# Two heads of a pair in the two 64-row halves of the array, and one VectorE instruction for the maxima of both

## The reference

```python
q = (x @ Wq).reshape(B, S, 16, 16).transpose(0, 2, 1, 3)
c_kv = x @ Wkv_down                                   # latent of 64
k, v = heads(c_kv @ Wk_up), heads(c_kv @ Wv_up)
qf, kf = rope(q), rope(k)
scores = einsum('bhqd,bhkd->bhqk', qf, kf) / sqrt(16)
scores = where(causal, -inf, scores)
out = einsum('bhqk,bhkd->bhqd', softmax(scores), v)
```

## Time and profile before

| | |
|---|---|
| median of 3 runs | 789.13 us (788.01 to 790.67) |
| the profiled execution | 787.88 us, its span 786.1 us |
| TensorE busy (matmul) | 699.7 us, 89% |
| VectorE busy | 567.3 us, 72% |
| ScalarE busy | 397.4 us, 51% |
| 640 row-maximum reductions on VectorE | 346.6 us |
| 640 matmuls for the maxima, 640 for the scores | 237.0 and 244.9 us |
| 1280 records of the values | 134.1 us |

### The profile page before, as it was taken

One profiled execution on the slowest core, in us unless ns is written; L12 is line 12 of the kernel. 1 busy time (PEld: TensorE's weight loads), 2 busy tenths in 40 slices (PEclk: granted clock), 3 DMA queues, 4 the chain that ended last, 5 costly groups with the idle time before them and its releaser, 6 DMA issues.

```text
span 786.1 us, 13117 instructions
## 1 busy us (share of the span) xinstructions
PE 699.7 (89%) x4086; PEld 444.5 (57%) x4087; DVE 567.3 (72%) x1297; ACT 397.4 (51%) x848; POOL 240.3 (31%) x297
## 2 busy tenths in 40 slices
PE   3579899899999999999999999999979999999910
PEld 3456575565665556556654555554467777777710
DVE  6666679778879977787698888863687755555545
ACT  2225365455656666667666776766823232222204
POOL 6526173440072207010611000010147413333332
PEclk9759899899999999999999999999999999999965
DMA  4864315035015101500341265332332223333254
GB/s 138 204 172 109 83 43 148 24 103 119 1 42 148 56 1 41 121 2 1 93 89 65 65 215 189 126 97 57 87 98 102 90 83 95 108 108 108 87 187 160
DMA packets 45096, 75.94 MB, mean 97 GB/s; under 512 B 5695, under 2 KB 23359, under 8 KB 44863
## 3 DMA queue, kind: packets, MB, share of 16 engines
q1 hardware_dynamic: 37423, 57.55, 27.2%
q0 software_dynamic: 4896, 13.67, 5.0%
q10 hardware_dynamic: 2720, 4.00, 1.4%
HBM read 41.91 MB, written 32.93 MB: 95 GB/s over the span
## 4 chain that ended last, share of the span: by engine, by line
PE 70%; DVE 16%; DMA 4%; issue 4%; ACT 3%; ACTq 1%; POOL 0%; SPq 0%; POOLq 0%; DVEq 0%
PE banks_ps L1144 15%; PE banks_ps L1124 14%; PE banks_ps L1085 14%; PE banks_ps L1181 7%; DVE mx L1342 6%; PE banks_ps L1215 5%; PE banks_ps L1001 3%; PE banks_ps L1092 2%; PE banks_ps L1194 2%; DMA q_stack<-m_rows 2%; PE banks_ps L1228 1%; ACT probs L888 1%; PE banks_ps L1277 1%; PE banks_ps L1203 1%; DVE base L1809 1%
## 5 line engine op out<-in xcount | busy, mean ns | idle before, releaser
L1342 DVE TENSOR_REDUCE mx<-banks_ps 128x1 f32<-128x512 f32 (+3 forms) x640 | 346.6, 602 | 93.1 <-PE banks_ps L1085 50.1
L888 ACT ACTIVATE probs<-banks_ps 128x512 f32<-128x512 f32 (+3 forms) x640 | 304.1, 546 | 180.9 <-PE banks_ps L1124 166.6
L1124 PE MATMUL banks_ps<-q_stack,k_stack 98*128 98x512 f32 (+3 forms) x640 | 244.9, 399 | 15.5 <-ACT probs L888 7.2
L1085 PE MATMUL banks_ps<-k_stack,q_stack 96*128 96x512 f32 (+3 forms) x640 | 237.0, 400 | 7.3 <-DMA q_stack<-kq_split 3.4
L1085 PEld LDWEIGHTS banks_ps<-k_stack,q_stack 96*128 96x128 f32 x640 | 124.8, 198 | 82.0 <-DVE mx L1342 37.1
L1124 PEld LDWEIGHTS banks_ps<-q_stack,k_stack 98*128 98x128 f32 x640 | 122.4, 195 | 51.4 <-ACT probs L888 29.1
L741 POOL TENSOR_SCALAR_AFFINE_SELECT probs<-probs 128x512 f32<-128x512 f32 x64 | 41.0, 640 | 331.0 <-ACT probs L888 331.0
L1144 PE MATMUL banks_ps<-probs,v_ones 128*17 128x512 f32 (+3 forms) x1280 | 134.1, 536 | 1.0 <-POOL probs L741 1.0
L798 POOL DMA_INDIRECT token_y<-ys,dest x47 | 45.4, 966 | 79.2 <-DVE ys L1785 76.3
L1144 PEld LDWEIGHTS banks_ps<-probs,v_ones 128*17 128x17 f32 x1280 | 29.5, 97 | 64.9 <-issue 41.1
L1181 PE MATMUL banks_ps<-w_up_sb,xg_t 128*128 x188 | 63.8, 462 | 0.3 <-ACT xg_t L941 0.3
(11 more groups left out here) (186 smaller groups left out, 685.0 us busy)
## 6 DMA issues: line engine op xcount, KB each, us to landing
kq_split<-kq_stage SPq DMA_DIRECT2D x32, 256.0 KB, 3.4
k_stack<-kq_split SPq DMA_DIRECT2D x8, 768.0 KB, 6.6
q_stack<-kq_split SPq DMA_DIRECT2D x32, 192.0 KB, 6.1
xg<-slot_x SPq DMA_DIRECT2D x47, 130.0 KB, 2.1
slot_x<-blank SPq DMA_DIRECT2D x11, 520.0 KB, 6.9
w_up_sb<-w_up SPq DMA_DIRECT2D x16, 352.0 KB
kq_split<-kq_stage SPq DMA_DIRECT2D x32, 128.0 KB, 3.2
x_raw<-xT SPq DMA_DIRECT2D x4, 512.0 KB, 5.7
```

The lines of the kernel that those rows point to most:

```text
L888: nc.scalar.activation(probs[:, s % PROB_BUFS, h, off:CH], score_bank(n)[:, off:CH], ACT.Exp)\
L1085: ins = nc.tensor.matmul(dst[:, at:at + keys], q_stack[0:STACK, u % 4, h, tile * P:(tile + 1) * P], k_stack[0:STACK, pair, kb * CH + k0:kb ...
L1124: nc.tensor.matmul(score_bank(n)[:, off:CH], k_stack[:, 2 * g + h // 2, b * P:(b + 1) * P], q_stack[:, u % 4, h, off:CH], start=True, stop ...
L1342: last = nc.vector.tensor_reduce(mx[:, u % 2, h * TPC + tile, kb:kb + 1], bank_of(bank)[:, at:at + keys], AX.X, ALU.max)
```

## The change

Each head of a pair gets its own half of the partitions: the even head rows 0 to 49, the odd head rows 64 to 113 (48 rows, and 2 for the maximum). `q_stack` loses its zeros. The score matmuls of two neighbouring heads and the two matmuls for the maxima of two heads then use different halves of the array's rows. Banks for the maxima are handed out in pairs: the 576 banks become 288 pairs, each with two of the 4 turn banks; VectorE reduces a pair with one instruction if its two banks are neighbours, and with two if the pair wraps round (bank 3 and bank 0), which 81 of the 288 pairs do, since jobs take one bank and shift the count. A step issues half of its pairs, two scores, half of its jobs, and the same again.

```diff
-STACK = 2 * SPLIT
-ROWS = STACK + 2
+ROWS = SPLIT + 2
+HALF_ROWS = P // 2
...
-        filled.append(filled[-1] + BANKS_A_STEP[u // UNITS_PER_CHUNK])
+        filled.append(filled[-1] + BANKS_A_STEP[u // UNITS_PER_CHUNK] / 2)
...
+        wide = 2 if turn in max_no else 1
+        turn_banks[turn] = [(at + k) % TURN_BANKS if n < first_alone else LAST_MAX_BANKS + at % 2 for k in range(wide)]
+        turn_before[turn] = [user.get(bank) for bank in turn_banks[turn]]
+        user.update((bank, turn) for bank in turn_banks[turn])
+        at += wide
...
-                    sp.dma_start(k_stack[0:STACK, 4 * m:4 * m + 4, c * CH:(c + 1) * CH].bitcast(F32),
-                                 kq_dram[c, n - 1].rearrange("two copy (d j) n -> (two copy d) j n", j=GH)).then_inc(k_stacked, 16)
+                    for par in range(2):
+                        sp.dma_start(k_stack[half_rows(par, SPLIT), 4 * m:4 * m + 4, c * CH:(c + 1) * CH].bitcast(F32),
+                                     kq_dram[c, n - 1, par].rearrange("copy (d j) n -> (copy d) j n", j=GH)).then_inc(k_stacked, 16)
...
-            nc.gpsimd.memset(q_stack[0:STACK, 0:2].bitcast(F32), 0.0).then_inc(zeros_low, 1)
-            link(nc.gpsimd.memset(k_stack[STACK:ROWS, :, 0:CH].bitcast(F32), 1.0))
+            for par in range(2):
+                nc.gpsimd.memset(k_stack[HALF_ROWS * par + 32:HALF_ROWS * par + ROWS, :, 0:CH].bitcast(F32), 1.0).then_inc(ones_set, 1)
...
                 for tile, k0, keys, at in parts:
-                    ins = nc.tensor.matmul(dst[:, at:at + keys], q_stack[0:STACK, u % 4, h, tile * P:(tile + 1) * P],
...
+                    for par in range(2):
+                        ins = nc.tensor.matmul(bank_of(of, par)[:, at:at + keys],
+                                               q_stack[half_rows(par, SPLIT), u % 4, pair, tile * P:(tile + 1) * P],
+                                               k_stack[half_rows(par, SPLIT), stacked, kb * CH + k0:kb * CH + k0 + keys],
...
-                nc.tensor.matmul(score_bank(n)[:, off:CH], k_stack[:, 2 * g + h // 2, b * P:(b + 1) * P],
-                                 q_stack[:, u % 4, h, off:CH], start=True, stop=True).then_inc(pe_scores, 1)
+                nc.tensor.matmul(score_bank(n)[:, off:CH], k_stack[half_rows(h % 2), 2 * g + h // 2, b * P:(b + 1) * P],
+                                 q_stack[half_rows(h % 2), u % 4, h // 2, off:CH], start=True, stop=True).then_inc(pe_scores, 1)
...
-            nc.vector.memset(q_stack[0:STACK, 2:4].bitcast(F32), 0.0).then_inc(zeros_high, 1)
...
+                    b0, b1 = turn_banks[of]
+                    if b1 == b0 + 1:
+                        last = nc.vector.tensor_reduce(mx[:, u % 2, n:other + 1:other - n, kb:kb + 1],
+                                                       turn_ps[:, b0:b1 + 1, at:at + keys], AX.X, ALU.max)
+                    else:
+                        for k, to in enumerate((n, other)):
+                            last = nc.vector.tensor_reduce(mx[:, u % 2, to, kb:kb + 1], bank_of(of, k)[:, at:at + keys], AX.X, ALU.max)
```

More of the change, by code:

```diff
@@ L118, in build_program @@
         at = min(at, first_step[u] - MAX_AHEAD)
-        for bank in reversed(max_banks(u)):
+        for bank in reversed(max_pairs(u)):
             while at >= 0 and len(max_at[at]) >= room(at):
@@ L489, in score_bank, with bank_of, half_rows, mx_row_of @@
             return turn_ps[:, k - SCORE_BANKS]
-        def bank_of(turn):
-            return turn_ps[:, turn_bank[turn]]
+        def bank_of(turn, k=0):
+            return turn_ps[:, turn_banks[turn][k]]
+        def half_rows(par, rows=ROWS):
+            return slice(HALF_ROWS * par, HALF_ROWS * par + rows)
+        def mx_row_of(pair, par, tile):
+            return (par * (GH // 2) + pair) * TPC + tile
         def wait_read(eng, job):
@@ L1153, in run_banks @@
                         max_unit(bank[0])
-                    max_bank(bank)
+                    max_pair(bank)
             def before_scores():
@@ L1165, in _ @@
             for s in range(NS + 1):
-                banks, jobs = quarters(max_at[s]), quarters(aux_at[s], 2)
+                banks, jobs = quarters(max_at[s], 2), quarters(aux_at[s], 2)
                 for half in range(2):
-                    for h in (2 * half, 2 * half + 1):
-                        run_banks(banks[h])
-                        if s < NS:
-                            score_head(s, h)
+                    run_banks(banks[half])
+                    if s < NS:
+                        score_head(s, 2 * half)
+                        score_head(s, 2 * half + 1)
                     for job in jobs[half]:
@@ L1669, in _ @@
             for s in range(NS + 1):
-                banks, jobs = quarters(max_at[s]), quarters(aux_at[s], 2)
-                for k in range(4):
-                    for bank in banks[k]:
-                        reduce_bank(bank)
-                    if k % 2:
-                        for job in jobs[k // 2]:
-                            if job in by_dve:
-                                read_aux(job)
-                    norm_part(s, k)
+                banks, jobs = quarters(max_at[s], 2), quarters(aux_at[s], 2)
+                for half in range(2):
+                    for bank in banks[half]:
+                        reduce_pair(bank)
+                    norm_part(s, 2 * half)
+                    for job in jobs[half]:
+                        if job in by_dve:
+                            read_aux(job)
+                    norm_part(s, 2 * half + 1)
                 for u in range(UNITS):
```

101 lines of the change are left out of this document (48 added, 53 removed).

## The result

The changed kernel takes **878.61 us** (median of 4 runs, 872.86 to 879.11) against 789.62 us of the kernel before (788.01 to 790.67): ratio **1.111** [1.106, 1.116], 89 us slower. The profiled execution has a span of 877.4 us, 91.3 above the 786.1 of before.

The account below looks back on a forecast made before the run. TensorE was taken to set the pace, VectorE 15% behind. Units 8 to 14 -11, units 4 to 7 +2, prologue and units 0 to 3 -3, the rest 0: -12 from 787.9, so 776, 777 by the median; range 757 to 808.

Parts of the forecast that it names:

- forecast A: Whole kernel: the main forecast, 777 us, own range 766 to 787, chance 0.58.
- rival E: Attention: TensorE's granted clock falls behind waits, in a quarter of the 64 periods +37, about 813 us; chance 0.07.
- Jobs: Projections, outputs and VectorE's other work between pairs: gains and losses set against each other, 0, with 8 us either side.
- +2: Units 4 to 7: every other period has a fifth pair, 6.10 us against 5.99 before; 16 periods, +2 us.
- The steady period: Two attention steps in units 8 to 14: 5.53 us instead of 5.76, 48 periods, -11 us.
- Pair 4: Fourth pair of maxima banks in a period: waits for VectorE to finish pair 2, starts at V + 3.01.
- V: Start of the first pair behind the values, from which a period is counted; next period forecast at V + 5.49.
- a pair's two matmuls overlap: Maxima and scores in different halves run side by side: 0.25 us a pair, between 0.233 (full overlap) and 0.466 (none).
- the wide reduction: VectorE's one instruction for two banks, 1024 elements: 1.22 us; four pairs 4.56 us a period against 4.80.
- D: Rival: the halves do not overlap, a pair costs 0.466 us, period 6.03 us, 815 us in all; chance 0.11.
- Masks: Masking matmuls use all 128 rows: borders of 0.1 us each way, 19 us, against 17 given back; counted as 0.
- Prologue and units 0 to 3: Stages before unit 4: maxima of unit 0 -1 us, units 0 to 3 -2 us, together -3 us.

Follow-up runs that it names:

- e9: The change with full stacks of 96 and 98 rows instead of halves; pairs of banks, wide reduction and new order stay: 838.0 us, ratio 1.046.
- e10: The change's halves alone, with single banks, single reductions and the order of the kernel before: 939.5 us, ratio 1.163.
- e3: The kernel before, with matmuls for maxima and scores using only the first 48 rows of both stacks: 1038.4 us, ratio 1.292.
- e8: The changed kernel, halves padded with zero rows to 64 (maxima 62), plus five 64-row filler matmuls a period that add zero: 833.6 us, ratio 1.032.
- e14: Same kernel as e13, but both heads' matmuls go first, then both masks, and steps take an even number of banks: 812.1 us, ratio 1.027.
- e11: Same kernel as e10, with rows padded with zeros to 64 and five 64-row filler matmuls a period: 868.8 us, ratio 1.080.
- e13: Same kernel as e11 (halves of 64 rows, fillers, single banks), but in the change's order on TensorE: 862.0 us, ratio 1.093.
- e5: The changed kernel, each half padded with zero rows to 64 (maxima 62), no matmul or column added: 850.2 us, ratio 1.079.
- e4: The changed kernel with five more matmuls a period, 64 rows by 512 columns, adding zero: 848.1 us, ratio 1.054.
- e12: The kernel before with the change's order on TensorE alone; full rows, single banks and single reductions stay: 792.8 us, ratio 1.005.

## Why the prediction was wrong, point by point

- **The step that failed** is the clock. The sum of forecast A has no term for it: every stage keeps the clock of before. The fall was left to rival E, "the granted clock falls", with a chance of 0.07 and a price of +37. It rested on "the fall to 0.5 came behind waits", and took the change's 1.4 us of waits a period as the only reason. In units 4 to 7 TensorE is idle for 14.5 us in e9 and 16.1 in the change, and e9 has a clock of 0.94 there, the change 0.73; e10 and e3 hardly wait and lose it. (In units 8 to 14 e9 waits less than the change, 13.7 us against 24.1, so for them this comparison is weaker.) What the change did to the clock was halve the rows that each column uses, and let two heads take the time of one. The price was sized for a quarter of the periods; half of the full calls of values ran slow. The prediction's own sign for E, a clock column below 1.0 past 230 us, is what the profile after shows. With the clock back at 0.92 the same kernel is at 1.032, so about 8 of the 11 per cent are the clock (e8 also pays for its fillers, so this is a lower bound).
- **Jobs, and units 4 to 7.** "0, with 8 us to either side" and "+2". e8, which has the clock nearly back, takes 13.7 us more in units 4 to 7 and 9.0 more in 8 to 11; e14, which hands out single banks, takes 5.7 and 8.2 more. So pairs are worth at most 8 us in units 4 to 7 (part of it can be the clock, 0.92 and 0.96 there) and nothing that can be told in 8 to 11. The prediction counted in which waits jobs would fall, but not that a job leaves room for one pair only in four banks. The "+2" was also a slip: if only every other period has a fifth pair, its own 5.53 and 6.10 average 5.82 against 5.99, and 16 periods give -3. It moves the forecast by 5 us, inside its range.
- **The steady period.** 5.53 us forecast, 5.65 measured in undisturbed ones (e8: 5.64 to 5.69 in nine of them). Pair 4 starts at V + 3.11 (583.47 less 580.36; forecast 3.01), the values at V + 3.80 (3.60): the count was 0.1 us short up to pair 4 and 0.1 between it and the values. The forecast's end is unclear as well: V + 5.44 and 0.1 make 5.54, not 5.49. The gain on 48 periods is thus some 5 us and not 11, of which e8's units 12 to 14 show 0.9.
- **Right:** a pair's two matmuls overlap (0.23 to 0.25 us); the wide reduction takes 1.22 us and saves VectorE next to nothing; D didn't happen.
- **Masks.** "0.1 us each way" was about right: 0.10 to 0.14 between 64 and 128 rows. It counts little in the change, since the two masks of a pair stand together: the three periods take 6.67 or 6.68 us in e8, 6.54 to 6.56 before. It counts a lot in e11 and e13. The Trainium skill (TensorEngine Tiling (Array Packing), "Key Properties") says that a change of mode drains the array; that these borders cost 0.10 to 0.14 us each agrees.
- **Prologue and units 0 to 3.** -3 forecast; +2.7 and +12.8 measured, and in units 0 to 3 still +7.9 in e8 (69.8 against 61.9), where the clock is 0.83 against 0.91. e9 has +5.4 there at 0.92, with pairs; e14 has +7.2 at 0.79, without them. How much is pairs and how much the clock wasn't separated.

What stays open: why e10's clock is below that of the whole change; and where the 8 to 9 us of e14 and e8 in units 8 to 11 go, whether in fillers or in borders at the jobs.

## What to carry to other kernels

Two matmuls side by side in the halves of the array save time only if what they free isn't lost again: where both use half as many rows as before, check the granted clock of an experiment with fewer rows first. That costs one edit (e3), needs no new order, and would have told the sign here, though not the size (1.292 against 1.111). Where buffers are handed out in pairs, count the other users: with four buffers, one other user leaves one pair in flight. And group what needs the full array: each border with matmuls in halves cost 0.10 to 0.14 us here, and masks that stood one by one cost 50 us more than masks in twos (e13 and e14).

## What the runs showed of the hardware that wasn't expected

- The granted clock fell to 0.68 over 490 us in which TensorE was busy 99% of the time, by using 48 rows in place of 96 and 98 (e3; half of its matmuls for maxima and scores had zeros alone as queries).
- Rows whose products are all zero count as in use: 64 rows in place of 50 took the mean clock from 0.82 to 0.87 and the ratio from 1.111 to 1.079 (e5).
- Five matmuls a period that add zero made a kernel 30 us faster (e4, 848.1 against 878.6 us, on another chip), and 1.111 became 1.054.
- Two matmuls of 512 columns in the two halves take as long as one, 0.23 us, while a border between 64 and 128 rows costs 0.10 to 0.14 us (e13 against e12).
